# Cross-attention block on one NeuronCore: the opening of the kernel rebuilt, with new lists of steps

## What is computed

```python
mu  = jnp.mean(input, axis=(1, 2), keepdims=True)
var = jnp.var(input, axis=(1, 2), keepdims=True)
xn = (input - mu) * jax.lax.rsqrt(var + EPS)
xn = xn * gamma[None, :, None] + beta[None, :, None]
q  = jnp.einsum('oc,ncs->nos', Wq, xn) + bq[None, :, None]
kv = jnp.einsum('od,nds->nos', Wkv, context) + bkv[None, :, None]
# 8 heads of 64 channels; k and v are the halves of kv
att = jax.nn.softmax(jnp.einsum('nhqc,nhkc->nhqk', q * scale, k * scale), axis=-1)
y = jnp.einsum('nhqk,nhkc->nhqc', att, v)
out = jnp.einsum('co,nos->ncs', Wo, y_as_channels) + bo[None, :, None]
return input + out
```

## Time and profile before

| what | value |
|---|---|
| median of 3 runs | 236.93 us |
| lowest and highest | 236.78 and 237.16 us |
| time of the profiled execution | 238.32 us |
| its span | 235.3 us |
| its mean granted TensorE clock | 0.95 |
| TensorE busy, matmuls | 210.5 us, 89% |
| VectorE busy | 200.8 us, 85% |
| ScalarE busy | 184.0 us, 78% |
| GpSimd busy | 157.9 us, 67% |

### The profile page before, as it was taken

One profiled execution on the slowest core, in us unless ns is written; L12 is line 12 of the kernel. 1 busy time (PEld: TensorE's weight loads), 2 busy tenths in 40 slices (PEclk: granted clock), 3 DMA queues, 4 the chain that ended last, 5 costly groups with the idle time before them and its releaser, 6 DMA issues.

```text
span 235.3 us, 7252 instructions
## 1 busy us (share of the span) xinstructions
PE 210.5 (89%) x2543; PEld 182.5 (78%) x2543; DVE 200.8 (85%) x585; ACT 184.0 (78%) x373; POOL 157.9 (67%) x153
## 2 busy tenths in 40 slices
PE   6878577999996999999989999999999799999882
PEld 6767456887885888888868888888888688897761
DVE  4588867789897898999997989999999699999765
ACT  2356546799888788998989888989898689898880
POOL 5030434579679677797978877789787578787450
PEclk9967857799999999999999999999999999999997
DMA  5961146345465646656566556665746574543000
GB/s 143 293 235 35 34 109 148 72 110 116 109 144 128 155 106 146 138 130 154 134 156 142 133 117 157 141 142 121 172 96 152 126 174 114 135 98 82 15 2 22
DMA packets 31092, 29.04 MB, mean 123 GB/s; under 512 B 4241, under 2 KB 29841, under 8 KB 31057
## 3 DMA queue, kind: packets, MB, share of 16 engines
q1 hardware_dynamic: 30736, 28.20, 51.0%
q10 hardware_dynamic: 320, 0.40, 0.6%
HBM read 3.80 MB, written 1.05 MB: 21 GB/s over the span
## 4 chain that ended last, share of the span: by engine, by line
PE 67%; DVE 16%; issue 7%; ACT 6%; DMA 2%; POOL 1%; ACTq 0%; POOLq 0%; DVEq 0%
PE ps_sc L535 11%; PE ps_max L560 10%; PE ps_sc L536 9%; DVE neg_max L886 7%; PE ps_z L494 6%; PE ps_z L496 5%; PE ps_z L495 5%; PE ps_t L510 4%; PE ps_z L424 3%; PE ps_m L601 3%; PE ps_t L511 3%; DVE z_sum L902 3%; PE ps_m L602 3%; ACT p_full L675 2%; PE ps_m L473 2%
## 5 line engine op out<-in xcount | busy, mean ns | idle before, releaser
L766 POOL TENSOR_TENSOR p_lo<-p_full,p_hi 128x512 f16<-128x512 f32 x122 | 139.9, 1164 | 52.8 <-ACT p_full L675 52.2
L886 DVE TENSOR_REDUCE neg_max<-ps_max 128x2 f32<-128x512 f32 x128 | 85.9, 678 | 9.6 <-PE ps_max L560 9.5
L672 ACT ACTIVATE p_hi<-ps_sc 128x512 f16<-128x512 f32 x128 | 77.3, 604 | 18.9 <-PE ps_sc L536 18.6
L675 ACT ACTIVATE p_full<-ps_sc 128x512 f32<-128x512 f32 x128 | 78.1, 610 | 0.8 <-POOL p_lo L766 0.8
L535 PE MATMUL ps_sc<-t_a,c_seq 128*128 128x256 f32 x256 | 72.7, 305 | 5.1 <-issue 3.9
L536 PE MATMUL ps_sc<-t_b,c_seq 65*128 65x256 f32 x256 | 68.4, 287 | 0.0
L494 PEld LDWEIGHTS ps_z<-u_hi,p_hi 128*128 128x128 f16 x512 | 46.4, 97 | 13.3 <-issue 7.5
L535 PEld LDWEIGHTS ps_sc<-t_a,c_seq 128*128 128x128 f32 x256 | 50.1, 196 | 7.7 <-issue 6.4
L494 PE MATMUL ps_z<-u_hi,p_hi 128*128 128x65 f16 x512 | 53.0, 194 | 3.0 <-DVE p_lo L922 1.9
L495 PE MATMUL ps_z<-u_lo,p_hi 128*128 128x64 f16 x512 | 52.8, 192 | 0.0
L496 PE MATMUL ps_z<-u_hi,p_lo 128*128 128x65 f16 x512 | 52.7, 193 | 0.0
(11 more groups left out here) (107 smaller groups left out, 237.2 us busy)
## 6 DMA issues: line engine op xcount, KB each, us to landing
t_a<-t_a SPq DMA_DIRECT2D x90, 128.0 KB, 2.4
t_b<-t_b SPq DMA_DIRECT2D x30, 128.0 KB, 2.4
c_pad<-c_hi SPq DMA_DIRECT2D x30, 64.0 KB, 2.0
c_seq<-c_hi SPq DMA_DIRECT2D x15, 128.0 KB, 2.4
x_seq<-x_hi SPq DMA_DIRECT2D x15, 128.0 KB, 2.4
x_res<-x_tiles SPq DMA_DIRECT2D x4, 256.0 KB, 6.2
out<-x_res SPq DMA_DIRECT2D x16, 64.0 KB, 2.1
c_seq<-c_lo SPq DMA_DIRECT2D x15, 64.0 KB, 2.1
```

What stands on the lines that cost most here:

```text
L672: nc.scalar.activation(p_hi[:, buf, :, :].rearrange("p t s -> p (t s)"), scores, ACT.Exp).then_inc(act_phi, 1)
L675: nc.scalar.activation(p_full[:, head % 2, :], scores, ACT.Exp).then_inc(act_p, 1)
L766: nc.gpsimd.tensor_tensor(p_lo[:, buf, :, :].rearrange("p t s -> p (t s)"), p_full[:, head % 2, :], p_hi[:, buf, :, :].rearrange("p t s -> ...
L886: nc.vector.tensor_reduce(to, ps_max[:, unit % 2, :].rearrange("p (t s) -> p t s", t=KT), X, ALU.max, negate=True).then_inc(dve_max, 1)
```

## The change

The work of the opening is cut and moved:

- ScalarE evicts a with two instructions per bank into a new tile `a_own` (rows 0 to 63 and 96 to 127). GpSimd copies the 64 main rows twice into `a_hi`. VectorE makes the low part of a with one 128-row instruction per bank, bank 0 behind the variance, bank 1 behind the bias additions. The bias row is now spread over 32 rows with ones of 1/32.
- The exp table is loaded right behind the root. Normalisation of x for sample 0 is one instruction; the first x_hi, the first context piece and b (two copies of 64 rows) follow in ScalarE's prologue.
- The products for b are made once (64 rows), without the wait for the variance; b's maximum is reduced from PSUM. The maximum over the context is made in three pieces and joined. The two tops go through `ps_sc` instead of `ps_m`; both are broadcast and multiplied behind the broadcast, so that `u_bound` on one element goes.
- Tops are handled at steps -6 to -1 instead of 1 and 2. u of sample 0 is made at steps 2 and 3 instead of 3 and 4. The lists for x, context and rows of maxima are new: x of sample 1 is staged at step -8 (before -2), of sample 2 at -1 (before 3), context of sample 1 at -1 (before -4), and the first rows of maxima are sent at -6 ahead of it. Context pieces 3 and 4 are made by step 8 (before 53).
- Projection turn 3 waits for the bias additions, the second scores for the scale of u.

```diff
-T_FIRST = (0, 3, 3, 3, 4, 5, 6, 6, 6, 6, 6, 6, 6, 7, 7, 7, 7, 8, 8, 8, 9, 9, 9, 10, 10, 10)
...
-MAX_FIRST = (0, 0, 2, 3, 4, 6, 6, 8, 9, 10, 10, 13, 15, 16, 16, 18, 20, 20, 22, 22, 24, 25, 26, 27, 28, 29)
-AV_FIRST = (0, 0, 0, 0, 0, 0, 0, 0, 0, 0, 0, 0, 0, 0, 1, 2, 3, 3, 4, 4, 4, 5, 6, 6, 7, 7)
-U_FIRST = (3, 4, 7, 9)
-MT_FIRST = (-3, 0, 6)
-NEG_MAX_FIRST = (-2, 2, 7)
-X_STAGE_FIRST = (-2, 3)
-C_STAGE_FIRST = (-4, 3)
-B_EVICT_AT, EXP_TABLE_AT, B_HIGH_AT = -5, -7, 1
-BO_AT, C_TOP_AT, B_TOP_AT, TOP_AT, UNSCALE_AT, B_LOW_AT = -7, -8, -5, 1, 1, 3
-TOPS_AT, BOUND_AT = 1, 2
-POOL_XN_AT = (-7, -5, -2)
...
-X_HIGH_AT = (-7, -6, 0, 7, 21, 39, 57, 73)
-X_LOW_AT = (-4, 0, 8, 11, 25, 40, 58, 75)
-C_HIGH_AT = (-4, 1, 20, 52)
-C_LOW_AT = (-5, -1, 4, 22, 53)
...
+T_FIRST = (0, 0, 2, 3, 4, 4, 4, 5, 6, 6, 6, 6, 7, 7, 7, 7, 8, 8, 8, 8, 8, 9, 9, 9, 10, 10)
...
+MAX_FIRST = (0, 0, 2, 4, 4, 5, 6, 7, 9, 10, 11, 13, 15, 16, 17, 19, 20, 20, 22, 23, 24, 24, 26, 28, 28, 29)
+AV_FIRST = (0, 0, 0, 0, 0, 0, 0, 0, 0, 0, 0, 0, 0, 0, 0, 1, 2, 2, 3, 4, 5, 5, 5, 6, 6, 7)
+U_FIRST = (2, 3, 7, 8)
+MT_FIRST = (-3, 1, 6)
+NEG_MAX_FIRST = (-6, 0, 7)
+X_STAGE_FIRST = (-8, -1)
+C_STAGE_FIRST = (-1, 3)
+B_HIGH_AT = 0
+C_TOP_AT = (-8, -8, -7)
+TOP_AT, UNSCALE_AT, B_LOW_AT = -5, -1, 1
+TOPS_AT, BOUND_AT = -6, -4
+POOL_XN_AT = (-6, -2)
...
+X_HIGH_AT = (-5, 6, 10, 26, 39, 57, 73)
+X_LOW_AT = (-7, 0, 6, 15, 28, 40, 58, 75)
+C_HIGH_AT = (-7, -3, -1, 5)
+C_LOW_AT = (-4, -3, -1, 2, 8)
...
+BIAS = C + C // 2
...
             def products_b():
                 for h in range(H):
                     wv_h, wo_h = (w_sb[0:C, w + h * C:w + (h + 1) * C] for w in (W_V, W_O))
-                    for k in range(2):
-                        rows = slice(k * C, (k + 1) * C)
-                        mm(ps_sc[rows, 1, h * C:(h + 1) * C], wv_h, wo_h, start=True, stop=True)
-                        last = mm(ps_m[rows, BO_COL:BO_COL + 1], wo_h, w_sb[0:C, W_BV + h:W_BV + h + 1], start=(h == 0), stop=(h == H - 1))
+                    mm(ps_sc[0:C, 1, h * C:(h + 1) * C], wv_h, wo_h, start=True, stop=True)
+                    last = mm(ps_sc[0:C, 0, BO_COL:BO_COL + 1], wo_h, w_sb[0:C, W_BV + h:W_BV + h + 1], start=(h == 0), stop=(h == H - 1))
                 last.then_inc(pe_bw, 1)
...
-            pe.wait_ge(dve_var, 1)
             products_b()
...
-                    if part == 0:
-                        pe.wait_ge(dve_bo, 1)
-                    else:
+                    if part == 1:
...
-                        pe.wait_ge(act_ahi, 3 * (k // 2 + 1))
-                        pe.wait_ge(dve_alo, 2 * (k // 2 + 1))
+                        pe.wait_ge(pool_ahi, 2 * (k // 2 + 1))
+                        pe.wait_ge(dve_alo, k // 2 + 1)
+                    if turn == 3:
+                        pe.wait_ge(dve_bo, 2)
...
                     if m == 0 and head == 1:
-                        pe.wait_ge(act_b, 1)
+                        pe.wait_ge(dve_uscale, 1)
...
                 if n * H + h == TOPS_AT:
-                    pe.wait_ge(dve_tops, 2)
-                    pe.wait_ge(act_mt, 2)
-                    nc.tensor.transpose(ps_m[0:1, 0:P], tops[:, 0:1], ident[:])
-                    nc.tensor.transpose(ps_m[0:1, P:2 * P], tops[:, 1:2], ident[:]).then_inc(pe_tops, 1)
+                    pe.wait_ge(dve_ctop, 1)
+                    pe.wait_ge(act_b, 2)
+                    for a in range(2):
+                        last = nc.tensor.transpose(ps_sc[0:1, 1, a * P:(a + 1) * P], tops[:, a:a + 1], ident[:])
+                    last.then_inc(pe_tops, 1)
                 if n * H + h == BOUND_AT:
-                    pe.wait_ge(dve_bound, 1)
-                    mm(ps_m[:, S:S + 1], ones_row[:], u_bound[:], start=True, stop=True).then_inc(pe_bound, 1)
+                    pe.wait_ge(dve_top, 1)
+                    mm(ps_sc[:, 1, S:S + 2], ones_row[:], top[:], start=True, stop=True).then_inc(pe_bound, 1)
 
...
+                            pe.wait_ge(act_mt, 2)
...
-            def a_high(bank, to, rows):
-                nc.scalar.activation(to[:, bank * H // 2:(bank + 1) * H // 2, :].rearrange("p h c -> p (h c)"), ps_max[rows, bank, :],
+            def a_high(bank, rows):
+                nc.scalar.activation(a_own[rows, bank * H // 2:(bank + 1) * H // 2, :].rearrange("p h c -> p (h c)"), ps_max[rows, bank, :],
                                      ACT.Copy, scale=C ** -0.5).then_inc(act_ahi, 1)
...
-            act.wait_ge(pool_a0, 1)
             for bank in range(2):
                 act.wait_ge(pe_a, bank + 1)
-                a_high(bank, a_hi[0:C], slice(0, C))
-                a_high(bank, a_lo[C:C + 1], slice(C, C + 1))
-                a_high(bank, a_hi[C:P], slice(0, C))
+                a_high(bank, slice(0, C))
+                a_high(bank, slice(BIAS, P))
             act.wait_ge(dve_var, 1)
             nc.scalar.activation(root[:], var[:], ACT.Sqrt).then_inc(act_root, 1)
+            act.wait_ge(act_table, 1)
+            nc.scalar.activation(warm[:], ones_row[:, 0:1], ACT.Exp).then_inc(act_table, 1)
             act.wait_ge(dma_c[0], 16)
             nc.scalar.activation(c_seq[0:C, 0, :, :], ctx_raw[0:C, 0:1, :].broadcast_to([C, 2, S]), ACT.Copy).then_inc(act_c0, 1)
-            c_high(0)
             act.wait_ge(dve_scale, 1)
             act.wait_ge(dma_x[0], 16)
-            for slot in range(2):
-                nc.scalar.activation(x_seq[0:C, 0, slot, :], x_raw[0:C, 0, :], ACT.Identity, bias=xn_shift[0:C, 0:1],
-                                     scale=xn_scale[0:C, 0:1]).then_inc(act_x0, 1)
+            nc.scalar.activation(x_seq[0:C, 0, :, :], x_raw[0:C, 0:1, :].broadcast_to([C, 2, S]), ACT.Identity, bias=xn_shift[0:C, 0:1],
+                                 scale=xn_scale[0:C, 0:1]).then_inc(act_x0, 1)
+            act.wait_ge(pool_xn, 1)
+            nc.scalar.activation(x_hi[:, 0, :], xn[:, 0, :], ACT.Copy).then_inc(act_xhi, 1)
+            c_high(0)
+            act.wait_ge(dve_btop, 1)
+            for k in range(2):
+                nc.scalar.activation(b_sb[k * C:(k + 1) * C], ps_sc[0:C, 1, :], ACT.Copy).then_inc(act_b, 1)
...
-                if n * H + h == B_EVICT_AT:
-                    act.wait_ge(pe_bw, 1)
-                    nc.scalar.activation(b_sb, ps_sc[:, 1, :], ACT.Copy).then_inc(act_b, 1)
-                if n * H + h == EXP_TABLE_AT:
-                    act.wait_ge(act_table, 1)
-                    nc.scalar.activation(warm[:], ones_row[:, 0:1], ACT.Exp).then_inc(act_table, 1)
...
                 if (j := due(X_HIGH_AT, {}, n, h)) is not None:
+                    j += 1
                     if j < POOL_XN:
...
-            nc.gpsimd.memset(a_lo[C:P].bitcast(fp32), 0.0).then_inc(pool_a0, 1)
+            nc.gpsimd.memset(a_own[C:BIAS].bitcast(fp32), 0.0).then_inc(pool_a0, 1)
...
+            for bank in range(2):
+                pool.wait_ge(act_ahi, 2 * bank + 1)
+                heads = slice(bank * H // 2, (bank + 1) * H // 2)
+                for k in range(2):
+                    need(pool, pool_ahi, 2 * bank + k)
+                    nc.gpsimd.tensor_scalar(a_hi[k * C:(k + 1) * C, heads, :], a_own[0:C, heads, :].bitcast(fp32), 1.0, 0.0, ALU.mult,
+                                            ALU.add).then_inc(pool_ahi, 1)
+            pool.wait_ge(pool_ahi, 2 * 2)
             pool.wait_ge(dve_scale, 1)
+            normalise(0)
 
...
-            def a_low(bank, to, hi):
-                dve.wait_ge(act_ahi, 3 * (bank + 1))
+            def a_low(bank):
+                dve.wait_ge(act_ahi, 2 * (bank + 1))
+                dve.wait_ge(pool_a0, 1)
                 heads = slice(bank * H // 2, (bank + 1) * H // 2)
-                nc.vector.scalar_tensor_tensor(out=a_lo[to, heads, :].rearrange("p h c -> p (h c)"), in0=ps_max[to, bank, :],
-                                               scalar=C ** -0.5, in1=hi[:, heads, :].bitcast(fp32).rearrange("p h c -> p (h c)"),
+                nc.vector.scalar_tensor_tensor(out=a_lo[:, heads, :].rearrange("p h c -> p (h c)"), in0=ps_max[:, bank, :],
+                                               scalar=C ** -0.5, in1=a_own[:, heads, :].bitcast(fp32).rearrange("p h c -> p (h c)"),
                                                op0=ALU.mult, op1=ALU.subtract).then_inc(dve_alo, 1)
 
-            main, main_hi = slice(0, C), a_hi[0:C]
-            bias, bias_hi = slice(C + 32, C + 33), a_lo[C:C + 1]
-
-            nc.vector.memset(x_seq[C:P, :, 1, :].bitcast(fp32), 1.0).then_inc(dve_ones, 1)
+            nc.vector.memset(x_seq[C:P, :, 1, :].bitcast(fp32), 1.0 / (P - BIAS)).then_inc(dve_ones, 1)
             nc.vector.memset(c_seq[C:P, :, 1, :].bitcast(fp32), 1.0).then_inc(dve_ones, 1)
             nc.vector.memset(b_w[C:P, 1, :].bitcast(fp32), 0.0).then_inc(dve_ones, 1)
+            nc.vector.memset(tops[C:P, 1:2], 0.0).then_inc(dve_ones, 1)
+            chain(nc.vector.memset(tiny[:], 1e-30))
...
-            a_low(0, main, main_hi)
...
+            a_low(0)
```

(34 more changed lines are left out.)

30 lines of the change are left out of this document (16 added, 14 removed).

## The result

The median went from 236.94 us (236.78 to 237.16, four runs) to 230.83 (229.03 to 231.67, four): 6.1 us less, a ratio of 0.9753, interval 0.9711 to 0.9795. I had forecast 229.6, 7.3 less. A ratio takes only executions within 1.5% of the fastest of their kernel, so it can differ from the ratio of two medians. The profiled execution is the fastest of the four, 229.03, with a span of 227.2.

What follows compares the result with a forecast made beforehand. TensorE works nearly throughout from 62.4 us, so the question was how much earlier the opening hands over. Sample 2 starting 7.3 us earlier, with 172.9 us unchanged behind it, takes the median from 236.93 to 229.6; range 227.8 to 233.6.

Steps and rivals of the forecast that it cites:

- 1, 3. Statistics, copies on GpSimd: Opening: `mu` at 10.75, scale ready at 14.97 instead of 15.53; four GpSimd copies of 0.69 us, nobody else waiting.
- 2. Table load: Opening, ScalarE: the load behind the root takes 1.28 us, costs 0.1 there and frees 1.5 where it was.
- 4. Products for b: Opening, TensorE: half of 64 matmuls last 1.0 to 1.8 us, end by 15.2; first projection at 16.15, 2.1 earlier.
- 5. VectorE to sample 0: VectorE up to the first scores: its shortened list lets sample 0's scores start at 26.5 instead of 30.2 us.
- 6. SyncE: SyncE's queue: first maximum of sample 1 until 28.3, second head 28.7; rows of sample 1 issued no earlier than 38.5.
- 7. Clock and steps: Steps 1 to 15: clock back at about 34.3; sample 1 starts at 41.9, 7.5 earlier, sample 2 at 55.1, 7.3 earlier.
- (b): Opening: the clock returns by 28 to 31 us and SyncE's queue becomes the bound; 1.3 us better, 228.3; chance 0.12.
- (a): Opening: clock low until 41 to 44 us, steps 4 to 7 cost 2 to 3 us more, 232.1; chance 0.22.
- (c): Handovers among five queues, mainly at SyncE's staging of sample 2, add waits; half the gain goes, 233.3; chance 0.13.
- (d): Sample boundaries behind 60 us: slower landings of rows of maxima, 1.8 us at five more, 9 us lost, 238.6; chance 0.06.

Runs made afterwards that it cites:

- e1_copies_wait: Changed kernel with GpSimd's four copies of the high part of a waiting for the variance; 231.32 us, ratio 0.9724 to the kernel before.
- e3_table_late: Changed kernel with the exp table loaded at ScalarE's step -6 instead of behind the root; 233.45 us, ratio 0.9787 to the kernel before.
- e7_vector_more: Changed kernel with two useless 128x512 reductions added on VectorE at step -4; 230.99 us, ratio 0.9694 to the kernel before.
- e8_stage_both: Changed kernel with contexts of samples 1 and 2 staged at steps -7 and -6 instead of -1 and 3; 229.46 us, ratio 0.9686.
- e4_before_filled: Kernel before with eight idle matmuls ahead of projection turn 4; 232.94 us, ratio 0.9842.
- e5_after_filled: Changed kernel with three idle matmuls, one before sample 0's first maximum, two before the tops; 229.39 us, ratio 0.9634 to the kernel before.
- c_after: The changed kernel, unchanged, timed and profiled again (the second profile); 231.32 us, ratio 0.9799 to the kernel before.

## Why the prediction was right, and where it was not

The sign, the size (6.1 of 7.3 us) and the place are as forecast: all in the opening, 172.6 us behind it. On the way there several steps did not hold, and two of the errors met. Point by point:

**1, 3. Statistics, copies on GpSimd.** `mu` at 10.91 and the copies (0.66 us each, 0.69 forecast) came right; the scale did not, 15.49 for 14.97. The step that failed is "Nobody else waits for GpSimd here". Nobody is seen to wait for it, but some small VectorE instructions beside the copies take 0.48 for 0.20 and 0.76 for 0.33 (`e1_copies_wait`). A gain of 0.56 us was 0.04, and 0.27 in the second profile. The end of the copies was also summed wrongly: 9.95 and four times 0.69 make 12.7, not 13.3, and they ended at 12.73.

**2. Table load.** 1.28 us, as the trace of before had it, and not the 2.7 that the Trainium skill, "ScalarE: Activation LUTs", section "Table sets: the hidden batching unit", has for a switch; the next activation starts 0.01 us behind the load. It cost nothing that can be seen (`e3_table_late`, by its marks). The normalisation ended at 16.34, 0.7 late: it started 0.5 late, with the scale, and took 0.81 us where I had 0.6.

**4. Products for b.** The failed step is "half of the 64 matmuls last 1.0 to 1.8 us by the two levels". They take 3.5 at the lower level and 2.8 with the clock falling among them. I had divided a duration by a count; in the old kernel instructions that wrote rows 0 to 63 and rows 64 to 127 ran side by side. They ended at 15.35 and 16.00. In the second profile this held the first projection (17.62 for 16.15), through the maximum of b and the long L845. In the first it did not: there the maximum of b was done at 16.08, and VectorE waited 0.30 us more for the late normalisation, so that the 16.89 is the error of points 1 and 2.

**5. VectorE to sample 0.** 27.34 and 28.79 for 26.5: 0.74 and 1.47 of that were there at the first projection, and 0.56 more in the second profile is the long L851. VectorE is the chain (`e7_vector_more`). `u_bound` now takes 0.14 (L868), and its 1.02 us did not turn up elsewhere.

**6. SyncE.** The first maximum of sample 1 at 28.70 (28.3), the second head at 29.01 (28.7), the rows issued at 40.00 (39.8): right. But I had the rows ready at 39.3 and the queue free at 38.5; they were ready at 38.81 and the queue free at 40.00, so it held them for 1.2 us. The landing then took 2.4 us where I had 1.9. With the queue out of the way the two boundaries are 0.25 to 0.75 us shorter (`e8_stage_both`).

**7. Clock and steps.** The clock came back at 23.7 (24.8), not at 34.3: the clock of rival (b), ten microseconds early, without (b)'s time, since VectorE binds there and not TensorE. The marks are 42.53 and 44.34 for 41.9, 54.64 and 56.62 for 55.1. From sample 0 to 1 I had 15.4 us with the lower clock for half of it, and it took 15.19 and 15.55 with the full clock: the clock bought next to nothing there. From sample 1 to 2 I had 13.2 us, by VectorE's list, and it took 12.11 and 12.28, with TensorE as the bound: of that list, one low part of u, one of t and part of the sums of z were already done before sample 1 started. So I was 0.84 us late at sample 0 and won 1.1 behind sample 1; that the first profile's 54.64 lies so near 55.1 is two errors that met. The other thing that I mis-sized is the clock of before: `e4_before_filled` takes 3.3 to 4.1 us from the old order by it. How much of the change's own gain is the clock isn't shown.

**The rivals.** (a) fell by the granted clock. With it falls what I had hung on the Trainium skill, "TensorE: Matmul & The Clock Gate", section "What's actually happening", that idle time behind the products would keep the clock low: TensorE was idle 1.3 of the 10 us from 13.7 to 23.7, and the clock came back. (c) is true for 1.2 us of queue and for the b maximum, and not for half of the gain. (d) did not come: at first scores behind 50 us TensorE idles 4.7 us in three places, 3.9 in three before. The slow landing that it feared does occur: before sample 4 the rows took 3.9 us to land, in the second profile 1.9.

```profile
PE ps_sc L538 <- issue: 4.7, 3, 2.0
```

**A version that beats both.** `e5_after_filled` and `e8_stage_both` have medians 1.4 to 1.9 us below the changed kernel. Neither was compared with it directly, only each with the kernel before. The interval of `e5_after_filled` lies below both of the changed kernel's, that of `e8_stage_both` overlaps the first. But so low a ratio, 0.9694, also came from `e7_vector_more`, which only adds work. That each beats the kernel before is shown; that they beat the changed one is not.

**Left open:** what spreads executions of one kernel over 4 to 7 us. The profiles show three sources: how long the clock is low, whether L845 and L851 meet GpSimd (0.9 us), and landings of rows of 3.9 instead of 1.9 us (from sample 3 to 4 it took 13.81 and 11.64 us in the two profiles of one kernel). What decides each of them isn't known. Open too is why `e3_table_late` has a high median on early marks, and `e7_vector_more` a low one on late marks.

## What to carry to other kernels

A duration divided by a count is only a price if the instructions ran one after another: look whether the removed half ran beside the kept one. Before an opening is rebuilt, fill its idle TensorE time with matmuls that nobody reads; in the old opening that alone took 1.6% off, where the whole change took 2.5%. On a queue that works in order, move an issue to where the queue is idle, and never put one that must wait ahead of those that needn't.

## What was not expected of the hardware

Pairs of 64x64 products that wrote the lower and the upper 64 rows of a bank took 0.43 us a head for four matmuls; two matmuls a head, of one half alone, took 0.43 as well, both at a granted clock of 0.50. At 1.00 the two took 0.23 (12.71 to 12.95 us in the changed kernel).

A VectorE instruction on SBUF that starts while GpSimd is in one can last until GpSimd's ends. In `e1_copies_wait` L837, L840 and L842 start within the second, third and fourth copy and end at 14.39, 15.18 and 15.89; these copies end at 14.38, 15.15 and 15.86. In the changed kernel L818 and the second of L822 end at 12.07 and 12.75, two copies at 12.03 and 12.72. In `c_after` L845 and L851 end 0.28 us behind GpSimd's subtractions. Those that start before GpSimd's instruction or in the gap of about 0.1 us between two copies keep their 0.17 us (L838, L841). L836 starts together with a copy and keeps it too, and so do, started beside GpSimd, the low part of a, which reads PSUM (0.69 at 17.19 in the changed kernel), and the reductions of the context (L858; 0.42, 0.94 and 1.21 us in both profiles of the changed kernel). The order of the starts thus explains all the slow ones in these profiles. It is read from them, and no run moved the starts alone; which kinds of instruction are spared is known only for these.

The same program on the same inputs had its clock low for about 10 us in one execution and about 13.5 in another, from 13.3 and from 11.6 us on, and its first scores 1.45 us apart.
